# Routed blocks that run on from chunk to chunk, results scattered straight to token order, and nine chunks in place of eight, in a gated attention and mixture-of-experts kernel

## What is computed

```python
# x, ctx: (128, 64, 128), one row is one token
def xattn(q, k, v):                       # 16 heads of 8 numbers, inside a token
    scores = einsum('bsqd,bskd->bsqk', qh, kh) / sqrt(8)
    scores = where(tril(ones(16, 16)), scores, -1e18)
    return einsum('bsqk,bskd->bsqd', softmax(scores), vh)
x = x + tanh(g_xattn) * xattn(layernorm(x), ctx, ctx)
h = layernorm(x)
shared = (silu(h @ sw1) * (h @ sw3)) @ sw2            # 128 -> 256 -> 128
rw, sel = top_k(h @ router_w.T + experts_bias, 2);  rw = softmax(rw)
moe = sum over the two: rw * ((silu(h @ w1[e]) * (h @ w3[e])) @ w2[e])
x = x + tanh(g_ffn) * (moe + shared)
```

## Time and profile before

| | |
|---|---|
| median of 3 runs | 789.05 us (787.27 to 798.73) |
| span of the profiled execution | 657.5 us, 12740 instructions |
| own time of the profiled execution | not given beside its span; the median less the span is 131.55 us |
| busy | PE 499.6, DVE 508.4, POOL 438.7, ACT 269.6 us |
| mean granted TensorE clock | 0.924 of 2.4 GHz |
| DMA | 109.30 MB, 166 GB/s over the span |

### The profile page before, as it was taken

How to read it: one execution, slowest core, us unless ns; L and a number is a source line. 1 busy time by engine, 2 the same in 40 slices (tenths; PEclk the granted TensorE clock), 3 DMA queues, 4 the chain that set the end, 5 groups by cost and what they waited for, 6 DMA issues and landing times.

```text
span 657.5 us, 12740 instructions
## 1 busy us (share of the span) xinstructions
PE 499.6 (76%) x3625; PEld 451.6 (69%) x3625; DVE 508.4 (77%) x999; ACT 269.6 (41%) x658; POOL 438.7 (67%) x466
## 2 busy tenths in 40 slices
PE   0028384699899989798887989998589999989910
PEld 0005262599789888698677978886588888979910
DVE  3999889799999999689966999999589874412301
ACT  2020450175527542457127642763064627344410
POOL 5000538525708788888888788879888887787444
PEclk9999585799899989799978999999799999999965
DMA  7950123463658577757297568945576768599722
GB/s 241 222 66 0 65 57 111 144 195 110 202 153 258 111 197 186 200 133 198 84 269 197 118 198 236 240 122 166 134 200 135 226 168 228 139 270 284 236 80 68
DMA packets 109457, 109.30 MB, mean 166 GB/s; under 512 B 10312, under 2 KB 80208, under 8 KB 109392
## 3 DMA queue, kind: packets, MB, share of 16 engines
q1 hardware_dynamic: 90160, 91.64, 49.2%
q0 software_dynamic: 18944, 16.86, 12.9%
q10 hardware_dynamic: 288, 0.00, 0.0%
HBM read 80.71 MB, written 29.84 MB: 168 GB/s over the span
## 4 chain that ended last, share of the span: by engine, by line
POOL 38%; PE 22%; DVE 14%; issue 12%; DMA 7%; ACT 6%; SPq 2%; POOLq 0%; DVEq 0%; ACTq 0%
POOL rows_in L570 18%; POOL xo L602 11%; PE ps_g L998 7%; PE ps_o L941 5%; PE ps_y L1025 4%; DVE prod L653 3%; POOL pv L594 3%; ACT xn L851 3%; PE ps_g L985 3%; DVE sc L658 2%; POOL rstd L544 2%; DMA rows_out<-yr 2%; DVE pv L685 2%; DMA xr<-rows_in 1%; PE ps_o L954 1%
## 5 line engine op out<-in xcount | busy, mean ns | idle before, releaser
L570 POOL DMA_INDIRECT rows_in<-xn,idx x128 | 182.1, 1422 | 40.9 <-issue 40.9
L998 PE MATMUL ps_g<-xrT,wq 128*128 128x128 f32 x1472 | 188.9, 284 | 1.9 <-ACT xrT L897 1.9
L998 PEld LDWEIGHTS ps_g<-xrT,wq 128*128 128x128 f32 x1472 | 180.9, 200 | 2.1 <-ACT xrT L897 2.1
L602 POOL DMA_INDIRECT xo<-rows_out,idx x96 | 153.8, 1602 | 29.1 <-issue 28.1
L794 DVE TENSOR_TENSOR eo<-sil,ps_g 128x512 f32<-128x512 f32 (+1 forms) x128 | 84.3, 664 | 90.0 <-ACT sil L889 83.9
L1025 PE MATMUL ps_y<-w2s,eo 128*128 (+1 forms) x992 | 136.1, 280 | 18.8 <-DVE eo L794 11.1
L1025 PEld LDWEIGHTS ps_y<-w2s,eo 128*128 128x128 f32 x992 | 125.2, 195 | 29.4 <-issue 23.6
L941 PE MATMUL ps_o<-pv,ident 128*128 128x512 f32 (+15 forms) x400 | 96.0, 394 | 46.2 <-DVE pv L685 36.0
L889 ACT ACTIVATE sil<-ps_g 128x512 f32<-128x512 f32 (+1 forms) x128 | 74.2, 585 | 96.3 <-PE ps_g L998 55.4
L941 PEld LDWEIGHTS ps_o<-pv,ident 128*128 128x128 f32 x400 | 64.3, 195 | 69.5 <-issue 56.9
L653 DVE TENSOR_TENSOR prod<-xn,ct 128x1024 f32<-128x1024 f32 (+15 forms) x128 | 90.7, 714 | 2.8 <-ACT xn L851 2.8
(11 more groups left out here) (87 smaller groups left out, 418.6 us busy)
## 6 DMA issues: line engine op xcount, KB each, us to landing
wq<-wall SPq DMA_DIRECT2D x184, 256.0 KB, 3.8
rows_out<-yr SPq DMA_DIRECT2D x88, 128.0 KB, 3.5
xr<-rows_in SPq DMA_DIRECT2D x40, 258.0 KB, 3.8
xt<-in_x SPq DMA_DIRECT2D x8, 512.0 KB, 4.8
ct<-in_ctx SPq DMA_DIRECT2D x8, 512.0 KB, 6.0
out<-xo SPq DMA_DIRECT2D x8, 512.0 KB
rows_in<-empty SPq DMA_DIRECT2D x2, 1483.5 KB, 20.8
wall<-in_L_ffn_w SPq DMA_DIRECT2D x2, 1024.0 KB, 12.2
```

What stands on the lines that cost most here:

```text
L570: pool.indirect_dma_start(rows_in[u % RI], bass.IndirectOffsetOnAxis(ap=idx[:, u % 3, k * TT + t:k * TT + t + 1], axis=0), xn2[:, c % XN, ...
L602: pool.indirect_dma_start(xo[:, c % XO, t], None, rows_out[u], bass.IndirectOffsetOnAxis(ap=idx[:, u % 3, at:at + 1], axis=0), compute_op= ...
L998: last = nc.tensor.matmul(ps_g[n % 2][:, q // HC, q % HC, a * P:(a + 1) * P], wq[:, b % WR, q * P:(q + 1) * P], xrT[:, i % 3, a * P:(a + 1 ...
```

## The change

The chunks are now 4, 8, 8, 8, 8, 8, 8, 8 and 4 tiles, in five sets: 0; 1 to 3; 4 to 6; 7; 8. In a set of several chunks the blocks of an expert run on: each expert has its own region of rows_in (SPAN blocks), a cursor (cur) and a mark of how many blocks are worked off (front). After a chunk that isn't its set's last, only as many blocks are worked off as must be full (sure, DONE); after the last, the rest. SP first writes an empty block behind each expert's last row (zero). The counts by chunk are 15, 9, 16, 30, 9, 16, 30, 23 and 15.

A row now carries a 130th number as well, its place in token order. Results aren't stored by block but scattered: POOL writes each block of results with an indirect DMA to ybuf in token order (post); empty rows fall outside and are dropped. A finished chunk is fetched from ybuf with two plain accumulating DMAs on POOL (accumulate), or, for the last three chunks, with two plain loads on SP (back) and added on DVE. SP loads rows and weights block by block (block_in). Additions of diagonals remain in chunks 4 to 8. PE sums the low and the high eight heads in separate banks, and att follows each. URG and AHEAD are other numbers.

```diff
-    TILE = [8, 8, 8, 8, 8, 8, 8, 8]
+    TILE = [4, 8, 8, 8, 8, 8, 8, 8, 4]
...
-    DW = D + 1
+    DW = D + 2
-    SETS = [[0], [1], [2], [3], [4], [5], [6], [7]]
+    SETS = [[0], [1, 2, 3], [4, 5, 6], [7], [8]]
...
+    def sure(c):
+
+        so_far = K * sum(TILE[a] for a in SETS[SET[c]] if a <= c)
+        return so_far + E - 1 if c in LAST else max(so_far - (E - 1), 0)
+
+    DONE = [sure(c) - (sure(c - 1) if c and SET[c - 1] == SET[c] else 0) for c in range(CHUNKS)]
...
-    XG, YR, WR, XN, XO, XT, PR, PV = 4, 6, 8, 3, 4, 1, 3, 6
+    YR, WR, XG, XN, XT, PR, PV = 6, 8, 16, 3, 1, 3, 6
...
-    ADDED = [[g for g in range(1, 8, 2)] if c > 0 else [] for c in range(CHUNKS)]
+    ADDED = [[] if c < 4 else [g for g in range(1, 8, 2)] for c in range(CHUNKS)]
...
+        URG = {('sp', 'load'): 5.5, ('sp', 'result'): 5.7, ('sp', 'block'): 3.0, ('sp', 'zero'): 3.3,
...
+            def block_in(b):
+                c, r = BLOCKS[b]
...
+                sp.wait_ge(s["tab"], c + 1)
+                at = sp.value_load(table[r:r + 1, c:c + 1], min_val=0, max_val=E * SPAN - 1)
                 if b >= WR:
                     sp.wait_ge(s["gu"], PLACE["R", RPAIR[BLOCKS[b - WR]]] + 1)
+                sp.dma_start(wq[:, b % WR], wall[bass.ds(at >> 7, 1)].rearrange("e p h -> p (e h)")).then_inc(s_wq[b % WR], 16)
+
+                sp.wait_ge(s_sc[c % 2], SCATTERED[c])
+                if c in LAST:
+                    sp.wait_ge(s["zeroed"], 16 * (1 + E * (SET[c] + 1)))
+                if b >= XG:
+                    before = RPAIR[BLOCKS[b - XG]]
+                    sp.wait_ge(s_ys[before % YR], 16 * posted(before))
+                sp.dma_start(xr[:, b % XG], rows_in[bass.ds(at * P, P)]).then_inc(s_xl[b % XG], 16)
+
+            def zero(u):
+
+                sp.wait_ge(s["rest"], u + 1)
+                for e in range(E):
+                    at = sp.value_load(rest[0:1, u, e:e + 1], min_val=0, max_val=(E * SPAN - 1) * P)
+                    sp.dma_start(rows_in[bass.ds(at, P)], empty[:]).then_inc(s["zeroed"], 16)
+
+            def back(c):
+
+                sp.wait_ge(s["o"], sums_to(CHUNKS - 1, NH))
+                for j, last in final_posts(c):
+                    sp.wait_ge(s_ys[j], 16 * posted(last))
+                for k in range(K):
+                    sp.dma_start(late(c, k).rearrange("p t d -> p (t d)"), results_of(c, k)).then_inc(s_back[c], 16)
...
+            def post(i):
+                c, r, w = RPAIRS[i]
+                pool.wait_ge(s["yev"], i + 1)
+                for a in range(w):
+                    pool.indirect_dma_start(
+                        ybuf, bass.IndirectOffsetOnAxis(ap=xr_i[:, BLOCK[c, r + a] % XG, D + 1:DW], axis=0),
+                        yr[:, i % YR, a], None, bounds_check=TRASH - 1, oob_is_err=False).then_inc(s_ys[i % YR], 16)
+
+            def accumulate(c, k):
+                if k == 0:
+                    pool.wait_ge(s["sh"], OFF[c + 1] // 2)
+                    for j, last in final_posts(c):
+                        pool.wait_ge(s_ys[j], 16 * posted(last))
+                need(pool, s_acc[c % 2], 16 * (K * (c // 2) + k))
+                pool.dma_start(xo[:, OFF[c]:OFF[c + 1]].rearrange("p t d -> p (t d)"), results_of(c, k), accum_op=ALU.add)\
+                    .then_inc(s_acc[c % 2], 16)
...
-                    nc.vector.tensor_tensor(paired(diag(pv, PV, m, g), n), by_head(ch)[:, :, 0:NH - g, :],
+                    nc.vector.tensor_tensor(paired(diag(pv, PV, m, g), n),
                                             ex[:, 0:n, g:NH, g].unsqueeze(3).broadcast_to([P, n, NH - g, HD]),
-                                            ALU.mult).then_inc(s["pv"], 1)
+                                            by_head(ch)[:, :, 0:NH - g, :], ALU.mult).then_inc(s["pv"], 1)
```

505 lines of the change are left out of this document (239 added, 266 removed).

## The result

The changed kernel takes 806.18 us in the median of four runs (801.37 to 809.87), the kernel before 788.16 of four (785.73 to 798.73): ratio 1.0254, 95% interval 1.021 to 1.0299. The forecast was 759 (738 to 804).

The account below looks back on a forecast made before the run. POOL was taken as the tightest bound in the middle: first scatter at 69, plus 456 to the last chunk's, 89 to the last post and 13 after, ends at 627; with 131.5 around the span, 759 us, range 738 to 804.

Parts of the forecast that it names:

- Time around the span: Outside the profiled span: 131.5 us between the 657.5 us span and the 789.05 us time, left unchanged.
- The start: Before the first scatter: half a chunk's DVE work, 24.4 us, goes, so the first scatter comes at 69.
- The price of a post: POOL's indirect DMA for each block of results: taken at 1.45 us, between 1.31 and 1.83; 1.31 in the tail.
- DVE's total: DVE's work over the whole kernel: 515 us after the change, from 508, so no lighter.
- PE was to be 17 us lighter: PE's work overall: 32 us less from 21 fewer blocks, 15 more from summing in place of additions, net 17 lighter.
- Sum 447, and 9 for the 2% that POOL idles now: POOL from first scatter to that of the last chunk: 447 us of work plus 9 idle, 456 in all.
- the slower rival: POOL stops behind posts waiting for yr: a chunk keeps 68 us, end at 681, time 812 us; chance 0.13.
- this could cost 9: Tail: SP's row loads and zero writes make 98 us against POOL's 89, so 9 us might be lost.
- SP 1.65 us a block: SP's loads for each block: 1.65 us where PE takes 1.5, counted at nothing until the tail.
- PE waiting for xr in the tail: Tail: named as a sign that the forecast is wrong, SP's loads leaving PE without rows; no size given.
- Fewer additions: Sums of a chunk: four and a half chunks with additions for seven, 9 us less DVE, 15 us more PE.
- Ninth chunk: First and last chunk of four tiles: first scatter 24.4 us earlier, against 8 us more DVE starts and two more norms.

Follow-up runs that it names:

- A: Kind of chip, or its condition that day, on which the kernel before took 661 to 667 us in the median of three sessions.
- B: Kind of chip, or its condition that day, on which the kernel before took 775 to 788 us in the median of three sessions.
- e9: The changed kernel again, no edit, on A: 686.96 us, where the kernel before takes 664.25, ratio 1.034.
- e2: The changed kernel with each of its nine chunks a set of its own, on A: 728.3 us, 1.102 to the kernel before.
- e12: The changed kernel with each post done twice, the second to a table nobody reads, on A: 825.0 us, 1.242 to the kernel before.
- e13: The changed kernel with only the first block of each pair posted, outputs lacking the routed part, on B: 761.09 us, 0.982 to the kernel before.
- e6: The changed kernel with order lists made as if posts could start 3 us after their yr, on B: 799.83 us, 1.031 to the kernel before.
- e14: The changed kernel with accumulating DMAs of 8 numbers a partition in place of whole rows, on B: 791.97 us, 1.022 to the kernel before.
- e15: The changed kernel with weight loads of 64 of 512 columns from the ninth block on, on B: 795.88 us, 1.027 to the kernel before.
- e16: The changed kernel with a pair's second block using the first's weights, 84 loads for 163, on B: 784.76 us, 1.013 to the kernel before.
- e3: The changed kernel with four additions in chunks 1 to 8, three chunks more, on A: 713.01 us, 1.079 to the kernel before.
- e18: The kernel before with nine chunks of 4, 8 (seven times) and 4 tiles, on A: 674.24 us beside 665.87, ratio 1.013.
- e7: The changed kernel with eight chunks of eight tiles, own sets, additions in chunks 1 to 7, on B: 836.18 us, 1.078 to the kernel before.
- e11: The changed kernel with the kernel before's URG and AHEAD where a stream's name exists there, on A: 711.74 us, 1.071 to the kernel before.

## Where the forecast went wrong

**Time around the span** (the forecast: "131.5 lies around it, and I leave that as it is"). Wrong: it is 1.7 to 1.8 us; the 20% between the profile's span and the times is what lies between A and B. The forecast's own relative statement, 627 of 657.5, is to be held against e9's 686.8. It misses by 60 us and in direction, so the base isn't the cause of the miss. That 759 and 806 lie only 47 us apart is no credit: 131.5 us that don't exist stand in the one, and the slower kind of chip in the other.

| step | forecast | e9 |
|---|---|---|
| first scatter | 69 | 61.6 |
| POOL's work a chunk (e9: from 205 to 545) | 59.6 | 59.8 |
| first scatter to that of the last chunk | 456 | 501.0 |
| from there to the last post | 89 | 114.4 |
| from there to the end | 13 | 9.8 |
| end | 627 | 686.8 |

**What held.** The start, from halving the first chunk. The price of a post: 1.17 + 0.30 = 1.47 in the stretch (taken at 1.45), 1.31 in the tail; its mean of 1.0 to 1.3 us busy (1.09). DVE's total, 509 for 515. That fewer blocks gain (e2: 1.48 us each). A scatter came out lower than its 1.74: 1.35 + 0.32 = 1.67 in the stretch. What did not hold beside the main step: PE was to be 17 us lighter and is 17 heavier (516.3 for 499.6). Its sums take 87.3 + 39.0 us where the forecast's additions gave 111, so the split by halves, counted at nothing, and the lower clock (0.90 for 0.92) are in it; how much each isn't shown. PE is busy for 405.7 of the 501 us of the middle, so it isn't taken for its pace.

**The step that failed: "Sum 447, and 9 for the 2% that POOL idles now."** The 447 is a sum from the first scatter to that of the last chunk; the 2% is from 205 to 545 us, where POOL was full. Over the whole middle it wasn't, in the kernel before already:

```profile
POOL msum L531 <- DVE stats L634: 29.3, 3, 17.1
POOL idx L560 <- DVE pos L779: 20.9, 2, 11.8
```

These are POOL's waits from 92 to 559.5 us (sum, times, longest), all of them before 205. In e9, from 61 to 562:

```profile
POOL msum L567 <- DVE stats L654: 42.2, 6, 32.2
POOL ybuf L612 <- ACT yr L935: 26.5, 9, 6.9
POOL scatter_pause L600 <- DVE idx L796: 7.0, 2, 4.7
```

| first to last positions | before | forecast | e9 |
|---|---|---|---|
| POOL waits for statistics and positions (DVE) | 50 | 9 in all | 49 |
| POOL waits for yr | 0 | | 27 |
| the rest, its work | 417 | 447 | 425 |
| together | 467 | 456 | 501 |

So POOL waits 76 us, not 9, and works 22 less than was summed; the two errors partly cancel. With the kernel before's own 50 us the sum would have been 497, four from the measured 501. The 49 us are mostly one place: behind a first chunk of four tiles POOL has eight scatters and some posts, while DVE has a full chunk's attention to do, and does it for 58.9 of 62 us. The row is the next norm on POOL:

```profile
103.98 0.70 POOL L567 TENSOR_TENSOR msum<-stats 128x8 f32<-128x8 f32 x1 [32.19 <-DVE stats L654]
```

That is why the half chunk at the start gains nothing for POOL: DVE works 433.0 us in this middle (434 in the forecast), POOL some 425, so POOL does not lead.

The 27 us on yr are new. POOL's gathers were asked for a whole set at a time and could wait in its queue: POOL had work whatever the others did. A post can only run behind its own yr, so POOL became one station of a ring, in which each waits for the one before: SP loads rows, PE and ACT work the block, POOL posts it, and only then SP may fill the row slot again. It is the mechanism of the slower rival (its chunk keeps 68, its end 681), to which the forecast gave 0.13 since "POOL is behind, not ahead, if my sum holds". POOL is both in turn: behind during a chunk's sixteen scatters, ahead after them. The longest chunk, 80.3 us, shows the first half. Its scatters run from 311 to 345 us, the posts stand behind them in POOL's order, and from 300 to 352 us others wait for posts:

```profile
SPq L472 <- DMA ybuf<-yr,xr: 25.6, 2, 23.7
```

```profile
ACT yr L935 <- DMA ybuf<-yr,xr: 10.1, 1, 10.1
PE ps_y L1056 <- ACT yr L935: 8.6, 2, 7.4
```

Another place shows the way through SP. SP, then PE, on the timeline; the last columns say what the engine waited for:

```profile
443.42 0.34 SPq L465 DMA_DIRECT2D wq<-wall  x1
447.04 0.34 SPq L473 DMA_DIRECT2D xr<-rows_in  x1
```

```profile
450.29 0.31 PE L1004 MATMUL ps_r<-ident,xr 128*128 128x128 f32 x1
456.57 0.48 PE L1004 MATMUL ps_r<-ident,xr 128*128 128x128 f32 x1 [5.97 <-DMA xr<-rows_in]
```

Between the two rows of SP it waits 3.1 us for a post that POOL issued at 439.5 and that landed at 446.8; it holds the row slot, since the post reads its index there. The row load then lands 9.5 us later, as xt, ct, a store and three accumulations were issued from 436 to 446 (DMA share 1.05 from 445 to 455), and PE stands still for 6 us. Here the post took POOL its usual 1 us, and 7.4 to land. From 205 to 545 SP waits 31.2 us for posts in four places, so the sixteen slots named as a reason against this rival do run out.

How far is this shown? The waits are read from the trace. That they cost their length is not shown. e12 is the nearest trial on A: with every post doubled the middle grows by 89 us, and outside the first chunk POOL's waits for others fall from some 37 us to some 5. So POOL had slack, and without it becomes the pace. e13 shows that posts matter on B, and that they aren't the pace there. e6, e14, e15 and e16 show that no single one of the part of POOL's wait that e6 took away, the accumulations' bytes, the weights' bytes and half of SP's weight loads sets the middle on B (587 to 595 in all four). What would bring the chunk to 60 us stays open, and so does whether the ring weighs the same on A, where only e12 of these was run. Two trials were not run: posts later in the lists on A, and the changed kernel with a first chunk of eight tiles, which would show what the 32 us at the start are worth.

**Tail: "this could cost 9", counted at nothing.** It costs 25. SP writes eight empty blocks (565.0 to 573.5) while the last scatters run, and from then on to 661.4 it waits only once, 5.0 us at 620. A block takes 1.73 us of it:

```profile
580.34 0.33 SPq L465 DMA_DIRECT2D wq<-wall  x1
580.94 0.33 SPq L473 DMA_DIRECT2D xr<-rows_in  x1
582.07 0.33 SPq L465 DMA_DIRECT2D wq<-wall  x1
```

The last row load is issued at 661.4, the 42nd: 73 us for the blocks themselves, the rest for stores, loads back and that wait. Between, there is one jam. The windows on A:

```profile
581.00:601.00 20.00, 18.07 (x139) 16.90 (x138) 3.44 (x5) 6.84 (x18) 12.55 (x14) 0.91 0.78 210
601.00:621.00 20.00, 10.27 (x62) 9.37 (x61) 4.47 (x7) 3.86 (x10) 7.77 (x8) 0.77 1.02 279
621.00:641.00 20.00, 18.79 (x143) 17.97 (x142) 3.74 (x6) 8.28 (x24) 10.91 (x11) 0.89 0.79 229
```

and the issues of 600 to 622 (KB, us to landing):

```profile
wq<-wall SPq DMA_DIRECT2D x10, 256.0 KB, 6.3
xo<-ybuf POOLq DMA_DIRECT2D x3, 512.0 KB
pv<-ybuf SPq DMA_DIRECT2D x2, 512.0 KB, 6.0
xr<-rows_in SPq DMA_DIRECT2D x10, 65.0 KB, 6.2
```

A set of three finishes at once, so results of its chunks 4 to 6 are fetched here together; 256 KB that land in 3.0 us in the median of the run take 6.3, and PE loses 8 us. That it loses them to this is read from the trace on A, not tried. The sum "SP 1.65 us a block" was near (1.73); the fault was to weigh it against POOL's 89 us as the larger of two numbers, where it adds its zero writes, the waits of a jam and PE's way behind the last load. e16 confirms SP's part on B (7 us), e15 denies that of the weights' bytes there. The forecast's own sign, PE waiting for xr in the tail, came: 17.8 us in ten places.

**Fewer additions: 9 us of DVE for 15 of PE, a net of little.** Too small: e3 puts additions back in three chunks and takes 26 us more. 13.6 of them lie in the intervals that hold the additions, about what DVE does more; the other half came later, in the middle and the tail, and its cause isn't shown. The Trainium skill's rule (SBUF — State Buffer, Who interferes with whom), that a DVE instruction with two SBUF inputs contends with GpSimd reading SBUF, would have the additions lengthen the scatters beside them; e3 doesn't show it, since those 40 scatters take 58.5 us with them and 58.1 without.

**Ninth chunk: 24 us less at the start.** True at the start (30.5 with all that changed, 27 in e18), and worth nothing in the total: the half chunk that leaves the start stands in the middle (e18), and POOL waits beside it for DVE.

So on either kind a large loss stands (e7: 60 us, mostly in how results and rows travel, though the table, the split sums and the orders are in it too) against gains from the sets (e2: 41), the additions (e3: 26) and the orders (e11: 12 to 25). The parts were measured on different kinds, e7's alone on B, and don't add up to the 19 to 23 us found.

## What to carry to other kernels

A share of idle time holds for the stretch in which it was read: 2% in the full part of a stage was 11% over the whole of it (50 of 467 us), 41 us that this forecast left out. An engine that is full because it has a backlog keeps its pace only as long as the backlog is there: whoever turns batched work into work for each block makes the engine a link of a ring, and should price the ring (slots, queue order, landing) beside the engine. Work that leaves a first stage comes back in the steady one if all of it still has to be done. When a variant lengthens one kind of instruction, look where the longer ones stand before naming the cause. And before any sum, a profile's span is to be held against the times beside it: 20% between them was no overhead here.
